# A fused graph and feed-forward kernel on one core: one-hots split over two engines, dead tiles dropped, loads and gathers started early

## The chip, the cores and the metric

The kernel runs on 1 core of one Trainium2 chip. The metric is the device time in microseconds (us) of one execution, from which the profile's span (first to last instruction) differs by the little that lies around it. Engines are named as in the profile: PE is TensorE, DVE VectorE, ACT ScalarE, POOL GpSimd, SP SyncE, which here only issues DMAs. ScalarE's and VectorE's instructions run in order on each engine, and the engines meet at semaphores and at a barrier between stages.

## The reference, cut to what matters

625 nodes with 768 features, 10000 edges sorted by destination, 34 relations. Four residual layers follow each other, each on a layer norm of the running `x`:

```python
x = x + gat_layer(elu(gat_layer(layernorm(x), heads=8)), heads=1)      # attention over all edges of a node
x = x + moe_ffn_0(layernorm(x))                                        # 8 experts, top 2
agg  = segment_sum(x[src], edge_type * n + dst); cnt = segment_sum(ones, ...)
mean = agg / maximum(cnt, 1)
h1   = einsum('rni,rio->no', mean, W_rel) + x @ W_root + b_rgcn        # x: layernorm(x)
xw   = h1 @ W_gcn                                                      # graph convolution:
x = x + dinv * segment_sum((xw * dinv)[src], dst) + xw * dinv**2 + b_gcn
x = x + moe_ffn_1(layernorm(x))                                        # 8 experts, top 2
```

The arithmetic on the weights is float16 in two parts: each float32 operand is cut into a high part and the rest ("hi" and "lo"), and each product is three products.

## The kernel before, in words

The 625 rows stand as NT = 5 tiles of 125 partitions. The stages follow each other with a barrier between them (`end_phase` or a block's end). Their starts, in us of the span, stand in the table of the next section.

**Edge stage** (`edge_phase`). The edges stand as 125 partitions x 80 columns. For each of 80 columns DVE makes two one-hots of 625 (`oh_s` from the sources at L207, `oh_d` from the destinations at L208, both in `hots`), in rings of HOTS = 8 that PE frees (`hots_free`), and PE (L352, L355, in `column`) multiplies them into a 625x625 matrix of edge counts and a count for each node and relation. Between the one-hots DVE works out where each edge goes (L223 to L286): the place of each edge in tiles of 128 edges, sorted by relation, with a second edge of the same pair beside the first (`ranks_ready` at L286). POOL then scatters one record for each edge column to DRAM (`scatter_records`, L392): TABLED_FIRST = 54 of the 80 in this stage, the others in the next. When PE's products are done, DVE stores counts (L291 to L294), makes the tables that steer the relation loop (L297 to L314: relation of each tile, whether a tile is the first of its relation, number of live turns), then masks (L318) and degrees (L319).

**Attention** (`gat_project`, `gat_attend`, twice). In the first projection SP loads the scattered records back when all 80 are written (L646), PE transposes them before its output tile 3 (`between`, L402), and DVE makes index columns from them (`slot_columns`). POOL gathers inverse counts beside all of the attention stages.

**The helper `Transposed`** is used in five places: for each row tile DVE normalises it (L517; for the norm it first takes `bn_stats` of all ten half tiles, L497), ACT writes the high part (L534), DVE the low part (L520), PE transposes both (L547), and ACT and DVE copy the result (L488, L486), in turns.

**Relation block** (`project_block` "q1", `relation_phase`, `gcn_phase`). q1 computes x @ W_root + bias; SP meanwhile stores the normalised rows to DRAM (`xn_dram`, L1845) and clears the accumulators. The relation loop then runs over tiles of up to 128 edges, in turns of UN = 4 tiles of which `live_turns` skips those that are dead as a whole. For each tile POOL gathers the rows of the edges' sources (L1559, L1561; AHEAD = 4 tiles ahead), PE sums rows of a tile that share a place (`mean`, L1700) and multiplies with the relation's weights (L599), ACT scales the result by the inverse count (L1628), POOL scatter-adds it to DRAM (L1579). A relation's weights (2304 KB) come through `wstage`, of two slots, and are cut into a ring by ACT (L1599) and DVE (L1640) at the first tile of the relation before. SP first waits for the first four gathers (L1537), then loads relation 1 (L1538). Relation 0 is loaded and cut already in q1 (`beside`). At the end SP loads both accumulators back (`load_sums`, 20 DMAs, L1867) before the stage may end. In `gcn_phase` DVE adds the halves (L510), PE multiplies with W_gcn and with the count matrix, and beside that the first weights of the last layer are merged in six chunks (`MergedFirst`: load, POOL L1463, DVE L1468 and L1470, ACT L1479, DVE L1474, which lets SP load the chunk after the next).

**Feed-forward layers** (`ffn_phase`, 0 and 1): router, gates, then up and down products.

## Time and profile before

| | |
|---|---|
| median of 3 runs | 1664.31 us (1662.63 to 1666.99) |
| the profiled execution | 1662.9 us, its span 1660.7 us |
| busy share of the span | PE 80%, PE weight loads 59%, DVE 56%, POOL 38%, ACT 32% |
| mean granted TensorE clock | 0.866 |

| stage | starts at, us |
|---|---|
| edge | 0 |
| first projection | 190.4 |
| rest of the attention | 254.2 |
| feed-forward 0 | 538.1 |
| q1 (root projection) | 729.6 |
| relation loop | 787.6 |
| graph convolution | 1356.8 |
| feed-forward 1 | 1452.8 |

How to read it: the busy shares are means over stages with different limits. In a timeline of an engine each row is one or more instructions, and the time in brackets behind it is the idle time before it and what ended that. An instruction's duration overlaps the next one's start on DVE and ACT by about 0.1 us, so a step is taken from start to start.

### The profile page before, as it was taken

The page shows a single profiled execution, that of the slowest core. Times are in us where ns is not written, and L with a number is a line of the kernel's source. Part 1 is how long each engine was busy: PE and PEld are TensorE (multiplying, and loading weights), DVE is VectorE, ACT ScalarE, POOL GpSimd, SP SyncE. Part 2 cuts the span into 40 slices and gives each one's busy share as a digit, 9 for nine tenths or more (in the row PEclk, how much of TensorE's full clock was granted, in tenths as well). Part 3 has the DMA queues.
Part 4 walks back from the last instruction along what each step waited for, and adds up shares of the span by engine and source line. Part 5 has one row for each costly group of instructions (what it writes and reads, how often), then busy time and mean ns, then how long its engine had stood idle before and what let it go on. Part 6 is the DMA issues. An engine that isn't in the chain of part 4 may idle for free. (4 is left out here: it accounts for less than half of the span.)

```text
span 1660.7 us, 30695 instructions
## 1 busy us (share of the span) xinstructions
PE 1335.1 (80%) x9640; PEld 982.2 (59%) x9641; DVE 935.8 (56%) x1711; ACT 535.8 (32%) x800; POOL 631.6 (38%) x751
## 2 busy tenths in 40 slices
PE   8699385792738489968599999999999938748988
PEld 6477365792634456856366666666666627435666
DVE  8953768685543644034266666566665536666810
ACT  0000320682320433013255554555555423122300
POOL 0077445776665000010355555555555522210000
PEclk9899685696769589988799999999999978958989
DMA  1000200000200421042699998899999865342301
GB/s 56 1 1 2 78 7 10 1 0 1 76 10 1 115 76 38 1 155 82 244 276 292 272 287 250 259 288 276 283 281 289 231 149 171 114 119 88 140 16 31
DMA packets 104209, 210.45 MB, mean 127 GB/s; under 512 B 23571, under 2 KB 48624, under 8 KB 104029
## 3 DMA queue, kind: packets, MB, share of 16 engines
q1 hardware_dynamic: 75484, 145.72, 25.5%
q0 software_dynamic: 28672, 64.04, 16.9%
q8 instruction: 32, 0.52, 0.1%
q14 instruction: 21, 0.16, 0.0%
HBM read 196.71 MB, written 37.22 MB: 141 GB/s over the span
## 5 line engine op out<-in xcount | busy, mean ns | idle before, releaser
L599 PE MATMUL r_pO<-ring,r_rowsT 128*128 x2592 | 433.1, 326 | 0.0
L599 PEld LDWEIGHTS r_pO<-ring,r_rowsT 128*128 128x128 f16 x2592 | 250.7, 98 | 158.4 <-issue 0.2
L1640 DVE SCALAR_TENSOR_TENSOR ring<-q_wstage,ring 128x768 f16<-128x768 f32 x198 | 175.2, 954 | 66.1 <-ACT ring L1599 61.9
L1579 POOL DMA_INDIRECT acc_dram<-r_msg,r_scol x72 | 133.0, 1847 | 167.0 <-PE r_pT L1700 98.0
L1599 ACT ACTIVATE ring<-q_wstage 128x768 f16<-128x768 f32 x198 | 148.8, 829 | 39.8 <-issue 25.0
L442 POOL DMA_INDIRECT inv_col<-qinv_dram,pair_col x112 | 120.0, 1072 | 79.3 <-POOL pair_col L455 74.4
L392 POOL DMA_INDIRECT slot_dram<-table_record,table_rowi x80 | 101.4, 1268 | 107.8 <-issue 107.2
L355 PE MATMUL acc<-oh_d,oh_s 125*125 125x512 f16 (+1 forms) x800 | 140.8, 316 | 0.0
L1628 ACT ACTIVATE r_msg<-r_pO,slot_inv 128x768 f32<-128x768 f32 x72 | 64.6, 897 | 191.6 <-PE r_pO L599 170.3
L1700 PE MATMUL r_pT<-r_S,q_parts 128*128 128x128 f16 x876 | 104.2, 222 | 24.2 <-DVE r_S L1657 12.6
L1647 DVE TENSOR_TENSOR r_rowsT<-r_pT,r_rowsT 128x512 f16<-128x512 f32 x73 | 50.2, 688 | 123.8 <-ACT r_rowsT L1608 111.7
L352 PE MATMUL acc<-R,oh_d 125*125 (+1 forms) x400 | 91.5, 229 | 18.8 <-DVE oh_d L208 18.8
L1700 PE MATMUL r_pT<-r_S,q_rows_b 128*128 128x128 f16 x876 | 104.3, 222 | 0.0
L887 PE MATMUL a_ps<-ident,cur 125*128 125x125 f32 x324 | 63.7, 371 | 49.0 <-ACT cur L861 23.5
L1559 POOL DMA_INDIRECT q_parts<-xn_dram,r_gcol x76 | 76.3, 1004 | 60.0 <-POOL r_gcol L1556 56.2
L1700 PEld LDWEIGHTS r_pT<-r_S,q_parts 128*128 128x128 f16 x876 | 70.8, 99 | 35.9 <-issue 27.9
L887 PEld LDWEIGHTS a_ps<-ident,cur 125*128 125x128 f32 x324 | 59.8, 286 | 52.8 <-ACT cur L861 23.2
L352 PEld LDWEIGHTS acc<-R,oh_d 125*125 125x125 f16 x400 | 56.3, 141 | 55.0 <-issue 19.3
L1561 POOL DMA_INDIRECT q_rows_b<-xn_dram,r_gcol x76 | 77.7, 1022 | 23.7 <-issue 23.1
L355 PEld LDWEIGHTS acc<-oh_d,oh_s 125*125 125x125 f16 x800 | 82.1, 144 | 0.0
L1329 DVE SCALAR_TENSOR_TENSOR x<-f_mps,x 125x384 f32<-125x384 f32 x20 | 10.2, 553 | 127.3 <-PE f_mps L599 127.3
L1556 POOL COPY r_gcol<-slot_idx 128x2 int32 (+1 forms) x76 | 58.0, 764 | 53.7 <-POOLq L1382 52.9
(359 smaller groups left out, 2421.0 us busy)
## 6 DMA issues: line engine op xcount, KB each, us to landing
q_wstage<-in_L_gnn_W_rel_dram SPq DMA_DIRECT2D x33, 2304.0 KB
f_stage<-in_L_ffn_w_dram SPq DMA_DIRECT2D x12, 768.0 KB, 5.1
stage<-in_L_gnn_W_dram SPq DMA_DIRECT2D x6, 768.0 KB
q_wstage<-in_L_ffn_w_fast_dram SPq DMA_DIRECT2D x6, 768.0 KB
q_wstage<-in_L_ffn_w_slow_dram SPq DMA_DIRECT2D x6, 768.0 KB
q_wstage<-in_L_ffn_h_fast_dram SPq DMA_DIRECT2D x6, 768.0 KB
f_stage<-in_L_ffn_w_fast_dram SPq DMA_DIRECT2D x6, 768.0 KB, 4.7
f_stage<-in_L_ffn_w_slow_dram SPq DMA_DIRECT2D x6, 768.0 KB, 6.2
```

Source lines behind the costliest of these rows:

```text
L352: eng.matmul(acc[0:P, 6, at:at + REL], oh_d[:, u, tile], onehot, start=False, stop=False, **kw)
L355: last = eng.matmul(a, oh_s[:, u, tile], oh_d[:, u, cols], start=False, stop=False, **kw)
L392: eng.indirect_dma_start(out=K.slot_dram, out_offset=bass.IndirectOffsetOnAxis(ap=K.table["rowi"][:, j:j + 1], axis=0), in_=K.table["recor ...
L442: eng.indirect_dma_start(out=got[:, u:u + 1], out_offset=None, in_=K.qinv_dram, in_offset=bass.IndirectOffsetOnAxis(ap=pair[:, u:u + 1], a ...
L599: ins = eng.matmul(out, x, w[:, h * n:(h + 1) * n], start=first and x is xh and w is wh, stop=last and x is xl, **kw)
L887: ins = eng.matmul(flat(bank)[:, lo:hi], bc(col[:, i:i + 1], [P, 128]), K.ident[0:P, off:off + hi - lo], start=True, stop=True)
L1559: eng.indirect_dma_start(out=rows[0][:, b, :], out_offset=None, in_=K.xn_dram, in_offset=bass.IndirectOffsetOnAxis(ap=gcol[:, b, 0:1], axi ...
L1561: eng.indirect_dma_start(out=rows[1][:, b, :], out_offset=None, in_=K.xn_dram, in_offset=bass.IndirectOffsetOnAxis(ap=gcol[:, b, 1:2], axi ...
L1579: eng.indirect_dma_start(out=K.acc_dram[u % 2], out_offset=bass.IndirectOffsetOnAxis(ap=scol[:, u:u + 1], axis=0), in_=msg[:, u, :], in_of ...
L1599: eng.activation(wring[:, slot, 0, k, :], wstage[:, slot, k, :], ACT.Copy, scale=W_SCALE).then_inc(s["w_hi"], 1)
L1640: ins_ = eng.scalar_tensor_tensor(wring[:, slot, 1, k, :], wstage[:, slot, k, :], W_SCALE, wring[:, slot, 0, k, :], ALU.mult, ALU.subtract)
L1700: last = eng.matmul(pT[b % 2][:, k // 4, (k % 4) * 128:(k % 4 + 1) * 128], rows[side][:, b, a * C + k * 128:a * C + (k + 1) * 128], S[:, b ...
```

## The change

Eight edits. (1) In the edge stage ACT makes `oh_d`, by a Square of (column number - destination) and a Relu of (1 - that), through a ring `apart` of four; DVE makes `oh_s` alone. The one-hots are spread differently between DVE's other steps, and the steering tables are made between one-hots, before the products end; degrees are reduced tile by tile; TABLED_FIRST is 46. (2) The live turns are two tiles and not four. (3) The statistics of the norm are taken by `measure` where rows of x are made (end of attention, of feed-forward 0 and of the graph convolution). (4) `Transposed` normalises tile i + 1 before it waits for tile i's high part. (5) Relation 1's and 2's weights are loaded, and the first four gathers made, in q1, where before they were made in the relation loop's stage. (6) `load_sums` loads tiles 0 and 1 in the relation stage and 2 to 4 in the next. (7) In the graph convolution the cuts of W_gcn stand between those of the rows on ACT and behind them on DVE. (8) The bias add of that stage goes from DVE to POOL.

```diff
-TABLED_FIRST = 54
+TABLED_FIRST = 46
@@ edge_phase, vector: hots
-                        eng.tensor_scalar(oh_s[:, u, :], iota_n[:, :], srcf[:, j:j + 1], None, ALU.is_equal)
-                        eng.tensor_scalar(oh_d[:, u, :], iota_n[:, :], dstf[:, j:j + 1], None, ALU.is_equal).then_inc(s["hots_ready"], 1)
+                        eng.tensor_scalar(oh_s[:, u, :], iota_n[:, :], srcf[:, j:j + 1], None, ALU.is_equal).then_inc(s["hots_s_ready"], 1)
...
-                hots(PREFIX_AT + 8, EJ)
+                hots(46, 52)
+
+                tg = c3[:, :].rearrange("p (t g) -> p t g", g=REL)
...
+                hots(60, EJ)
@@ edge_phase, scalar
+                def difference(j):
+                    eng.activation(apart[:, j % 4, :], iota_n[:, :], ACT.Square, bias=minus_dst[:, j:j + 1]).then_inc(s["apart_ready"], 1)
+
+                def hot(j):
+
+                    eng.wait_ge(s["hots_free"], j + 1)
+                    eng.wait_ge(s["apart_ready"], j + 1)
+                    eng.activation(oh_d[:, j % HOTS, :], apart[:, j % 4, :], ACT.Relu, scale=-1.0, bias=ones[0:EP, 0:1]).then_inc(s["hots_d_ready"], 1)
...
+                difference(0)
+                for j in range(1, EJ):
+                    difference(j)
+                    hot(j - 1)
@@ new
+def measure(K, eng, i):
+
+    for h in range(2):
+        last = eng.bn_stats(K.stats[:, i, h, :], K.x[:, i, h * HC:(h + 1) * HC])
+    return last
@@ Transposed.vector
+        prepare = add_halves if self.halves else normalise if self.norm else None
+        if prepare:
+            prepare(0)
         for i in range(NT):
-            if self.halves and i + 1 < NT:
-                add_halves(i + 1)
...
+            if prepare and i + 1 < NT:
+                prepare(i + 1)
             eng.wait_ge(s["hi_ready"], i + 1)
@@ relation_phase: live_turns, sync
-            turns = eng.value_load(K.live_row[0:1, TURNS:TURNS + 1], min_val=1, max_val=TURNS)
+            pairs = live_pairs(eng)
             with eng.Fori(1, TURNS) as i:
-                with eng.If(turns > i):
-                    for u in range(UN):
-                        step(i * UN + u, u, False)
+                for half in range(2):
+                    with eng.If(pairs > i * 2 + half):
+                        for u in (half * 2, half * 2 + 1):
+                            step(i * UN + u, u, False)
...
-            for b in range(AHEAD):
-                eng.wait_ge(gathered[b], 32)
-            load_w(eng, 1, 1)
-            with eng.Fori(1, REL // 2) as i:
+            eng.wait_ge(s["w_lo"], 2)
+            relation.load_w(eng, 3, 1)
+            with eng.Fori(2, REL // 2) as i:
...
-            load_sums(eng)
+            load_sums(eng, 0, 2)
@@ gcn_phase
+            load_sums(eng, 2, NT)
             eng.dma_start(bias[:, :], K.ins["L1_gnn_b_gcn"].partition_broadcast(P)).then_inc(s["bias_loaded"], 16)
...
-            merged.gpsimd(eng, 0, MERGE_CHUNKS)
+            merged.gpsimd(eng, 0, 2)
+            eng.wait_ge(s["bias_loaded"], 16)
+            eng.tensor_tensor(K.x[:, :, :], K.x[:, :, :], bc(bias[:, :].unsqueeze(1), [P, NT, C]), ALU.add).then_inc(s["bias_added"], 1)
+            merged.gpsimd(eng, 2, MERGE_CHUNKS)
...
-            W.scalar(eng)
-            T.scalar(eng)
+            T.scalar(eng, lambda i: W.scalar(eng, i, i + 1))
+            W.scalar(eng, NT)
@@ rgcn_phase: q1's sync and gpsimd
+            w_root.ready(eng, KC - 1)
+            relation.load_w(eng, 1, 1)
+            w_first.ready(eng, KC - 1)
+            relation.load_w(eng, 2, 0)
...
+            eng.wait_ge(s["dumped"], 48)
+            eng.wait_ge(s["extra"], 32)
+            T.wait_done(eng)
+            for b in range(AHEAD):
+                relation.gather(eng, b, b)
```

## Rows read from the trace of the kernel before

**Rows 1.** Relation loop: length, PE, PEld, DVE, ACT, POOL, PEclk, DMA, GB/s.
```profile
787.60:1356.80 569.20, 528.54 (x4418) 357.87 (x4418) 323.83 (x714) 273.65 (x416) 304.86 (x300) 0.97 0.90 265
```

**Rows 2.** Timeline of DVE, edge stage: start, duration, instruction, idle before.
```profile
84.72 0.24 DVE L286 TENSOR_TENSOR table_rowi<-place,beside 125x80 int32<-125x80 f32 x1
...
90.94 0.39 DVE L207 TENSOR_SCALAR oh_s<-iota_n,srcf 125x625 f16<-125x625 f16 x1 [0.70 <-PE acc L355]
...
154.91 0.38 DVE L207 TENSOR_SCALAR oh_s<-iota_n,srcf 125x625 f16<-125x625 f16 x1 [1.01 <-PE acc L355]
```

**Rows 3.** Timeline of PE, edge stage: a first product and the closing zeros.
```profile
9.36 0.76 PE L355 MATMUL acc<-oh_d,oh_s 125*125 125x512 f16 x2
...
168.19 1.68 PE L340 MATMUL acc<-zero 125*125 125x512 f16 x7
```

**Rows 4.** Timeline of ACT, attention: steps of 625, a table load.
```profile
300.67 1.28 ACT L847 ACT_TABLE_LOAD   x1
...
303.91 0.80 ACT L841 ACTIVATE t<-spread,al_s 125x625 f32<-125x625 f32 x1
304.62 0.71 ACT L847 ACTIVATE ex<-arg 125x625 f32<-125x625 f32 x1
```

**Rows 5.** Timeline of DVE (first three) and ACT (last), after the products.
```profile
171.59 4.06 DVE L297 TENSOR_TENSOR c<-iota_t,tin 128x3808 f32<-128x3808 f32 x1
...
183.30 2.58 DVE L318 TENSOR_SCALAR graph<-CT 125x625 bf16<-125x625 f32 x5
...
190.41 4.70 DVE L497 BATCH_NORM_STATS2 stats<-x 125x6 f32<-125x384 f32 x10 [1.09 <-PEq L90]
...
180.67 0.68 ACT L331 COPY CT<-acc 125x625 f32<-125x625 f32 x1 [1.00 <-PE acc L385]
```

**Rows 6.** Timeline of POOL: records scattered, the first, 54th, 55th and 80th.
```profile
85.98 4.61 POOL L392 DMA_INDIRECT slot_dram<-table_record,table_rowi  x1 [81.33 <-issue]
...
171.00 1.19 POOL L392 DMA_INDIRECT slot_dram<-table_record,table_rowi  x1 [0.31 <-issue]
...
191.27 1.19 POOL L392 DMA_INDIRECT slot_dram<-table_record,table_rowi  x1 [0.64 <-POOL h L653]
...
231.16 1.19 POOL L392 DMA_INDIRECT slot_dram<-table_record,table_rowi  x1 [0.30 <-issue]
```

**Rows 7.** Timeline of PE, first projection: transposes of the loaded tables.
```profile
236.36 0.74 PE L402 MATMUL g_ps<-ident,table_tables 112*128 112x112 f32 x4 [1.82 <-DMA table_tables<-slot_dram]
```

**Rows 8.** Timeline of ACT, feed-forward 0: the last copy of its row transposes.
```profile
559.01 1.48 ACT L488 COPY f_xT<-f_ps 128x750 f16<-128x750 f16 x2 [2.53 <-PE f_ps L547]
```

**Rows 9.** Timeline of DVE in q1, of POOL (fourth gather) in the loop.
```profile
768.48 1.83 DVE L1856 TENSOR_TENSOR q_h<-q_h,q_bias 125x768 f32<-125x768 f32 x2 [5.22 <-DMA xn_dram<-q_parts]
...
799.83 1.01 POOL L1561 DMA_INDIRECT q_rows_b<-xn_dram,r_gcol  x1 [0.30 <-issue]
```

**Rows 10.** Timeline of PE, relation loop: first row, third and last tile.
```profile
798.79 0.37 PE L1700 MATMUL r_pT<-r_S,q_parts 128*128 128x128 f16 x2 [10.90 <-DMA q_rows_b<-xn_dram,r_gcol]
...
829.58 6.16 PE L599 MATMUL r_pO<-ring,r_rowsT 128*128 x36
...
1334.48 6.01 PE L599 MATMUL r_pO<-ring,r_rowsT 128*128 x36
```

**Rows 11.** Timeline of SP's queue: the loads of the sums, first and last.
```profile
1347.95 0.83 SPq L1867 DMA_DIRECT2D q_h<-acc_dram  x2
...
1355.50 0.79 SPq L1867 DMA_DIRECT2D q_xn<-acc_dram  x2
```

**Rows 12.** Timeline of DVE and of POOL, graph convolution.
```profile
1378.34 4.15 DVE L1787 TENSOR_TENSOR x<-x,q_bias 125x3840 f32<-125x3840 f32 x1
...
1388.81 3.55 DVE L1474 SCALAR_TENSOR_TENSOR ring<-q_wstage,ring 128x1536 f16<-128x1536 f32 x1 [2.74 <-ACT ring L1479]
...
1387.99 2.75 POOL L1463 TENSOR_TENSOR q_wstage<-q_wstage,gate 128x1536 f32<-128x1536 f32 x1 [28.35 <-DMA q_wstage<-in_L_ffn_h_fast_dram]
```

**Rows 13.** Timeline of DVE, feed-forward 1: a wait for a load.
```profile
1483.72 0.55 DVE L1126 TENSOR_SCALAR f_b2p<-f_early 8x768 f16<-8x768 f32 x1 [7.92 <-DMA f_emb<-in_L_ffn_router_emb_dram]
```

209 lines of the change are left out of this document (119 added, 90 removed).

## The prediction, made before the changed kernel ran

> **What bounds the kernel now.** I read the windows by stage first, then each engine's timeline around the edits. In the edge stage one column of PE's products takes (154.91 - 90.94) / 38 = 1.683 us, and DVE waits for PE there [rows 2]; 80 columns are 134.6 us, yet the products end at 169.87 [rows 3], because earlier in the stage DVE's ranking steps starve PE. Behind them the stage lasts until 190.4, on DVE [rows 5]. In the first projection PE waits for tables that POOL's scatter delivers [rows 6, 7]. The relation loop is PE's, busy 528.5 of 569.2 us [rows 1], with 10.9 us lost at its start and more before its third tile [rows 10]. The stages around it are chains of small steps in which no engine is full: there each step on the chain costs its whole length.
>
> **Edge stage.** After the change PE is fed by DVE's one instruction and ACT's two a column. ACT's nearest rows of 625 elements start 0.71 us apart where the bias is a column [rows 4]; two are 1.42 us, below PE's 1.683, so PE sets the pace. The ring of 8 holds 13.5 us of PE's work, more than any of DVE's steps between two groups of one-hots. From the first product at 9.36, the products' end is 9.2 + 134.6 + 2.4 + 0.5 + 1.7 = 148.4: 2.4 for PE's half pace in the first 5 us (0.76 us a pair [rows 3]), 0.5 for the prefix products, 1.7 for the zeros. That is 21.5 us earlier. The table step from 171.59 to 183.30 [rows 5] moves between one-hots, where DVE has idle time. The masks then wait for the last count transpose, 181.35 - 169.87 = 11.5 us after the products [rows 5]; masks and degrees are 190.41 - 1.09 - 183.30 = 6.0 us for five tiles, so 1.2 follow the last. The next stage starts at 148.4 + 11.5 + 1.2 + 1.1 = 162.2, not 190.4: **-28.2**.
>
> **What POOL makes of that.** 80 records take (171.00 - 85.98) / 53 = 1.60 us each [rows 6]. ranks_ready at 84.96 [rows 2] comes at about 80: DVE saves 32 oh_d ahead of it and makes 14 oh_s more, and now sometimes waits for PE's ring (bounds 79 and 85). 46 records end at 81 + 46 x 1.6 = 155, hidden under 162.2 by 7 us; if that cover were gone, each us would count. In the projection 34 records and not 26 remain. The tables' transposes came 236.36 - 190.4 = 46.0 after the stage's start, 5.2 after the 80th record [rows 6, 7]; now 0.9 + 33 x 1.6 + 5.2 = 58.9: **+12.9**. PE's wait there grows from 1.8 to about 15 to 18 us, and after such a gap it starts at half pace: between 0 and the 2.4 above, I take 1.8. So 28.2 - 14.7 = **-13.5** for both stages: the edge stage's gain is given back in half, because POOL's chain of records only moves by its earlier start and by the shorter hole between its 54th and 55th (171.00 to 191.27).
>
> **Statistics and order of normalising.** The ten bn_stats are 4.70 us at the head of three stages [rows 5]. Moved, each tile's 0.94 lies under PE's products, except the last: +1.1 with its wait, three times. Feed-forward 0: the chain of transposes ended 559.01 + 1.48 - 538.1 = 22.4 us after the start [rows 8]. Without the statistics what is late next is ACT's table load of 1.28 [rows 4] (0.4 of it shows) and, before PE's first transposes, POOL's selection mask (it eats 1.3); the new order, in which the tile after is normalised while ACT writes this one's high part, gives 1.3 back. So 4.7 - 0.4 - 1.3 + 1.3: **-4.3** (bounds -3 and -6), +1.1 at the end of the attention. q1: 4.7 - 0.4 + 1.3, no mask: **-5.6** (bounds -4 and -6.5), +1.1 at feed-forward 0's end. Feed-forward 1: **0**, since DVE waits until 1483.72, 31 us into the stage, for a load that SP's queue delivers no sooner [rows 13].
>
> **q1 takes four gathers and two loads.** The rows' store lands at 768.5 [rows 9], some 5 us earlier once shifted; the four gathers take 800.84 - 787.6 = 13.2 us [rows 9] and end at 777 to 782, where q1 now ends at 782. Two loads of 2304 KB on SP's queue stand behind that store, not before it. Nothing shows: 0, bounds 0 and +5.
>
> **Relation loop.** The third tile's products began 829.58 - 787.6 = 42.0 us after the stage's start [rows 10], behind the gathers (10.9), the load of relation 1 that waited for them, and its cuts. With both there, the first products begin 5 us in (select, sums, cuts of the rows) and the third's two tiles on, at 19.6: **-22.4** (bounds -15 and -24). A tile is (1334.48 - 829.58) / 69 = 7.3 us [rows 10], tile 71 being the last. Counting the inputs as the kernel does gives 32 relations of two tiles and two of three: 70 live, so 35 pairs: **-14.6**. The second branch per turn lies under 36 queued products: 0. At the end 20 loads are issued in 8.3 us [rows 11]; eight take 3.3: **-5.0**.
>
> **Graph convolution.** DVE's first cuts of W_gcn go behind the rows, so PE's products start 4 us earlier (12 issues of loads now in front may take 1 back). What ends the stage is the chain of merged chunks: it loses the 4.15 us bias add [rows 12] and gains three statistics, 2.8, but starts 2.5 earlier, as W_gcn is cut earlier: **-3** (bounds -6 and +4). On POOL the add has 3840 columns, by the row of 1536 in 2.75 us [rows 12] 6.9 us. A row speaks against it: DVE's cut at 1388.81 takes 3.55 us and ends 1.6 us after POOL's multiply does [rows 12], so DVE stood still for POOL. The Trainium skill ("SBUF — State Buffer", section "Who interferes with whom") says that a DVE instruction with two SBUF inputs and a GpSimd one that reads SBUF exclude each other for the whole instruction; the trace agrees. One cut then waits up to 5 us, and the load it releases is needed only after PE's first products with the counts, so I count 0 for it.
>
> **Sum.** -28.2 + 14.7 + 1.1 - 4.3 + 1.1 - 5.6 - 22.4 - 14.6 - 5.0 - 3.0 = -66.2. Span 1660.7 - 66.2 = 1594.5; the profiled execution lay 2.2 above its span, and the median of the runs 1.4 above that: 1598, rounded down to 1597.
>
> **Rivals.** (A) Start of the relation loop: gathers, weight loads and the store of h1, which POOL's first scatter waits for, fall together; q1 ends 5 late and a third of the 22.4 is lost: 1597 + 5 + 7 = 1609. For it: the DMA share is 0.90 in the loop [rows 1]. Against: the window of q1 has queues free after the store. (B) ACT becomes the bound of the products: from a pair of 1.683 on. At 2.0 it is 80 x 0.32 = 25, in part under POOL: 1617. Against: [rows 4]. (C) POOL's bias add lies on the merge chain: +7 in place of -3: 1607. (D) Slower: Square and Relu do not share an activation table, and each column reloads twice: 2 x 1.28 + 1.42 = 3.98 us [rows 4], 80 x 2.3 = +184: 1781. It decides above 1.683 + 66 / 80 = 2.5 us a column, so one reload (2.70) is enough, 1678. No row shows a Square; for sharing speaks that Identity and Exp alternate after one load [rows 4]. The Trainium skill ("ScalarE: Activation LUTs", section "Table sets: the hidden batching unit") counts cheap functions such as relu in every set and doesn't name square there. (E) The pairs do nothing, as 71 or 72 tiles live: 1611.
>
> **Chances.** Forecast, 1589 to 1605: 0.62. Below 1589 (all upper bounds at once): 0.09. A 0.12, C 0.08, B 0.05, D 0.03, E 0.01. The range 1586 to 1614 leaves out D, most of B and the edge below. A measurement can tell 0.3% (5 us): faster 0.96, same 0.01, slower 0.03.
>
> **What would show it.** Right: products ending near 148 with PE's columns at 1.68 us, ACT's pairs at 1.4 and no table load between; the first projection starting at 162 and PE waiting 15 to 18 us for the tables; 70 scatters; the third tile's products 20 us into the relation loop; feed-forward 1 of unchanged length. Wrong: PE waiting for oh_d, DVE still for POOL in the graph convolution while a load is due, gathers landing after the loop's start.

## The result and the profile after

The changed kernel takes 1622.44 us (median of 4 runs, 1620.95 to 1628.56) beside 1665.65 us for the kernel before on the same chip: a ratio of 0.9748 with a 95% interval of 0.9717 to 0.9780. The profiled execution took 1621.38 us, its span is 1619.6 us, 41.1 less than before, where 66.2 were forecast. The time lies outside the range of 1586 to 1614.

The head of the page after, and the window of the relation loop (columns as in [rows 1]):

```profile
span 1619.6 us, 30896 instructions
PE 1317.4 (81%) x9518; PEld 968.5 (60%) x9519; DVE 919.3 (57%) x1626; ACT 649.5 (40%) x954; POOL 633.4 (39%) x744
771.98:1308.27 536.29, 513.72 (x4296) 347.50 (x4296) 319.50 (x700) 270.75 (x410) 290.11 (x280) 0.98 0.90 264
```

The same engines are as busy as before; ACT has gained 8 points of share from its one-hots. By stage (lengths in us; the last column is the best kernel of the experiments below, on another chip, in the longest of its six executions):

| stage | before | forecast change | after | change | combined kernel |
|---|---|---|---|---|---|
| edge | 190.4 | -28.2 | 160.7 | -29.7 | 162.8 |
| first projection | 63.9 | +14.7 | 78.6 | +14.7 | 66.2 |
| rest of the attention | 283.9 | +1.1 | 284.9 | +1.0 | 286.5 |
| feed-forward 0 | 191.5 | -3.2 | 190.0 | -1.5 | 190.0 |
| q1 | 58.0 | -5.6 | 57.8 | -0.2 | 54.7 |
| relation loop | 569.2 | -42.0 | 536.3 | -32.9 | 529.3 |
| graph convolution | 96.0 | -3.0 | 101.8 | +5.9 | 94.2 |
| feed-forward 1 | 207.9 | 0 | 209.5 | +1.6 | 212.0 |
| span | 1660.7 | -66.2 | 1619.6 | -41.1 | 1595.7 |

So the stages up to feed-forward 0 came out nearly as forecast, and four places behind them did not: the root projection, the start and the end of the relation loop, and the graph convolution. The lines follow, each answering to rows of before.

**Edge stage and first projection** (against [rows 3], [rows 4], [rows 6], [rows 7]). Timelines of PE, ACT (six rows), POOL and again PE:

```profile
144.22 1.68 PE L369 MATMUL acc<-zero 125*125 125x512 f16 x7
...
5.27 1.28 ACT L338 ACT_TABLE_LOAD   x1 [5.11 <-DVE minus_dst L219]
...
22.13 0.80 ACT L344 ACTIVATE oh_d<-apart,ones 125x625 f16<-125x625 bf16 x1
...
23.54 0.80 ACT L344 ACTIVATE oh_d<-apart,ones 125x625 f16<-125x625 bf16 x1
...
61.93 0.82 ACT L344 ACTIVATE oh_d<-apart,ones 125x625 f16<-125x625 bf16 x1
62.65 0.81 ACT L338 ACTIVATE apart<-iota_n,minus_dst 125x625 bf16<-125x625 f16 x1
63.62 0.82 ACT L344 ACTIVATE oh_d<-apart,ones 125x625 f16<-125x625 bf16 x1 [0.16 <-PE acc L385]
...
214.15 1.19 POOL L422 DMA_INDIRECT slot_dram<-table_record,table_rowi  x1 [0.30 <-issue]
...
219.47 1.02 PE L432 MATMUL g_ps<-ident,table_tables 112*128 112x112 f32 x4 [15.13 <-DMA table_tables<-slot_dram]
```

The products end at 145.9 and not at 169.9; there is one table load and none between Square and Relu. Early in the stage, while the ring of one-hots has free places, ACT takes 1.41 us from one Relu to the next (22.13 to 23.54); once the ring is full it takes 1.69 (61.93 to 63.62) and waits for PE in each. So PE sets the pace, with a margin of some 0.27 us, as worked out. The 80th record starts 53.5 us after the projection's start, and PE waits 15.13 us for the tables.

**Root projection** (against [rows 5]). Timelines of POOL and DVE at its head, two rows of after and three of before:

```profile
714.15 5.22 POOL L1912 MEMSET q_rows_b<- 128x6144 f16 x1 [185.17 <-POOLq L90]
...
714.89 4.50 DVE L539 TENSOR_SCALAR q_sd<-q_mv 125x5 f32<-125x5 f32 x1
```

```profile
729.62 5.22 POOL L1850 MEMSET q_rows_b<- 128x6144 f16 x1 [186.84 <-POOLq L90]
...
729.66 4.70 DVE L497 BATCH_NORM_STATS2 q_stats<-x 125x6 f32<-125x384 f32 x10 [0.99 <-PEq L90]
...
734.98 0.17 DVE L502 TENSOR_SCALAR q_sd<-q_mv 125x5 f32<-125x5 f32 x1
```

A DVE step on five columns takes 4.50 us and ends as POOL's memset does. Before, the ten bn_stats lay over that memset, in the same 4.70 us that they take without one, and the step on five columns came behind both, in 0.17 us. The bn_stats were taken away, and what they had covered is on the path.

**Start of the relation loop** (against [rows 10]). Timelines of PE, POOL and DVE from the fourth tile on:

```profile
800.00 6.01 PE L639 MATMUL r_pO<-ring,r_rowsT 128*128 x36
809.58 0.27 PE L1754 MATMUL r_pT<-r_S,q_parts 128*128 128x128 f16 x2 [3.58 <-DVE r_S L1711]
...
811.20 7.46 PE L639 MATMUL r_pO<-ring,r_rowsT 128*128 x36
...
791.58 1.64 POOL L1634 DMA_INDIRECT acc_dram<-r_msg,r_scol  x1 [12.47 <-DMA acc_dram<-q_h]
...
801.21 0.22 DVE L1721 SCALAR_TENSOR_TENSOR r_scol<-r_dup,row_move,row_base 128x1 int32<-128x1 f32 x1 [5.32 <-DMA acc_dram<-r_msg,r_scol]
802.65 5.34 DVE L1694 SCALAR_TENSOR_TENSOR ring<-q_wstage,ring 128x768 f16<-128x768 f32 x6 [1.23 <-issue]
```

The third tile's products begin 20.8 us into the stage (forecast 19.6). Then one step of PE is 11.20 us and the next 8.69, for 7.25: 5.4 us too much. Read backwards: PE waits for DVE's selection, which stands behind the cut of relation 2 at 802.65, which stands behind a column that waits for the landing of the first scatter, which waited 12.47 us for the store of h1.

**End of the loop** (against [rows 10], [rows 11]). Timelines of PE, POOL, SP's queue and DVE:

```profile
1284.44 6.01 PE L639 MATMUL r_pO<-ring,r_rowsT 128*128 x36
...
1292.35 1.62 POOL L1634 DMA_INDIRECT acc_dram<-r_msg,r_scol  x1 [2.29 <-ACT r_msg L1682]
...
1300.32 0.79 SPq L1934 DMA_DIRECT2D q_xn<-acc_dram  x2
...
1308.27 0.17 DVE L1837 TENSOR_SCALAR q_dinv<-deg 125x5 f32<-125x5 f32 x1 [20.25 <-PEq L1564]
```

SP has issued its eight loads by 1301.1, but the next stage starts at 1308.2. From the start of the last tile's product it is 23.8 us, where it was 22.3 with 20 loads: 12 loads fewer gained nothing.

**Graph convolution** (against [rows 12]). Timelines of POOL, DVE and PE:

```profile
1343.39 8.30 POOL L1814 TENSOR_TENSOR x<-x,q_bias 125x3840 f32<-125x3840 f32 x1
...
1343.53 9.78 DVE L1515 TENSOR_TENSOR q_wstage<-q_wstage 128x1536 f32<-128x1536 f32 x1 [2.71 <-POOL q_wstage L1508]
...
1355.81 7.74 PE L639 MATMUL n_ps<-q_gcn_parts,q_parts 128*125 128x384 f16 x36 [4.32 <-ACT q_xn L1829]
...
1394.63 8.28 PE L1870 MATMUL n_ps<-q_xn,graph 125*125 125x384 f32 x20 [3.08 <-DVE x L1852]
```

DVE's add, 1.76 us elsewhere, takes 9.78 us: it stands still for POOL's 8.30, and PE waits behind it. PE waits once more, 3.08 us, before its last tile, whose 20 products then take 8.28 us at a granted clock of 0.81; before they took 6.71 at 1.00, behind a wait of 0.25.

**Feed-forward 1** (against [rows 13]) still waits for the same load, now 11.84 us long:

```profile
1441.75 0.55 DVE L1168 TENSOR_SCALAR f_b2p<-f_early 8x768 f16<-8x768 f32 x1 [11.84 <-DMA f_emb<-in_L_ffn_router_emb_dram]
```

### The profile page after: what moved, and what is told of

Read it like the earlier page. It is cut to its first block and busy times, and to the rows that moved or that the text cites. A ratio compares the mean times of both kernels' runs of the same rounds, so it can differ in the third digit from the quotient of the medians.

```text
span 1619.6 us, 30896 instructions
## 1 busy us (share of the span) xinstructions
PE 1317.4 (81%) x9518; PEld 968.5 (60%) x9519; DVE 919.3 (57%) x1626; ACT 649.5 (40%) x954; POOL 633.4 (39%) x744
## 5 line engine op out<-in xcount | busy, mean ns | idle before, releaser
L639 PE MATMUL r_pO<-ring,r_rowsT 128*128 x2520 | 422.4, 327 | 0.0
L639 PEld LDWEIGHTS r_pO<-ring,r_rowsT 128*128 128x128 f16 x2520 | 244.2, 98 | 154.9 <-issue 1.5
L1634 POOL DMA_INDIRECT acc_dram<-r_msg,r_scol x70 | 131.0, 1871 | 152.5 <-PE r_pT L1754 101.8
L472 POOL DMA_INDIRECT inv_col<-qinv_dram,pair_col x112 | 120.1, 1073 | 79.2 <-POOL pair_col L485 73.6
L385 PE MATMUL acc<-oh_d,oh_s 125*125 125x512 f16 (+1 forms) x800 | 134.9, 308 | 0.0
L1754 PE MATMUL r_pT<-r_S,q_parts 128*128 128x128 f16 x852 | 100.4, 221 | 4.5 <-DVE r_S L1711 4.4
L927 PE MATMUL a_ps<-ident,cur 125*128 125x125 f32 x324 | 60.5, 358 | 50.9 <-ACT cur L901 24.2
L1754 PE MATMUL r_pT<-r_S,q_rows_b 128*128 128x128 f16 x852 | 100.5, 221 | 0.0
L1550 POOL DMA_INDIRECT q_parts<-xn_dram,q_gcol x74 | 74.4, 1005 | 57.2 <-POOL q_gcol L1546 55.5
L1552 POOL DMA_INDIRECT q_rows_b<-xn_dram,q_gcol x74 | 75.9, 1026 | 22.6 <-issue 22.6
L1912 POOL MEMSET q_rows_b<- 128x6144 f16 x1 | 5.2, 5217 | 185.2 <-POOLq L90 185.2
```

The source lines that it names most:

```text
L385: last = eng.matmul(a, oh_s[:, u, tile], oh_d[:, u, cols], start=False, stop=False, **kw)
L472: eng.indirect_dma_start(out=got[:, u:u + 1], out_offset=None, in_=K.qinv_dram, in_offset=bass.IndirectOffsetOnAxis(ap=pair[:, u:u + 1], a ...
L639: ins = eng.matmul(out, x, w[:, h * n:(h + 1) * n], start=first and x is xh and w is wh, stop=last and x is xl, **kw)
L927: ins = eng.matmul(flat(bank)[:, lo:hi], bc(col[:, i:i + 1], [P, 128]), K.ident[0:P, off:off + hi - lo], start=True, stop=True)
L1550: eng.indirect_dma_start(out=self.rows[0][:, b, :], out_offset=None, in_=self.K.xn_dram, in_offset=bass.IndirectOffsetOnAxis(ap=self.gcol[ ...
L1552: eng.indirect_dma_start(out=self.rows[1][:, b, :], out_offset=None, in_=self.K.xn_dram, in_offset=bass.IndirectOffsetOnAxis(ap=self.gcol[ ...
```

## The experiments

They ran on four chips, numbered 1, 4, 5 and 12 here; on which one the two kernels above ran is not known. The kernel before ran beside them each time, with medians of 1666.3 to 1676.9 us. The two kernels also went to chip 4, unaltered.

**The two kernels on chip 4.**

> The changed kernel unaltered, beside the kernel before, on the chip of these runs. Theory (this chip differs from the first in places that both kernels have): the edge stage's products end some 15 us later than 145.9, single tiles of the relation loop take 8.1 to 8.4 us for 7.25, the ratio is 0.98 and not 0.9748; the steps at the start of the relation loop (11.2 and 8.7 us), DVE's 4.50 us at the head of the root projection, the 23.8 us from the last tile's product to the graph convolution and its length of 102 us are the same as on the first chip. Rival (the experiments' own edits made the edge stage and the loop slower): 160.7 and 7.25 us again, 1622 us.

> The kernel before, unaltered, one look. If this chip is slower for PE while POOL scatters records, its edge stage is longer too, by less than the changed kernel's 15 us, as PE has 21 us of products less on its path there; the relation loop is 569 us or, where tiles take over 8 us, up to 585.

Measured: 1647.96 us (1629.67 to 1652.47) for the changed kernel, ratio 0.984 (0.977 to 0.991); the kernel before, profiled, has an edge stage of 204.0 us, 13.7 more than above, a loop of 570.1 and a graph convolution of 99.0, 3.0 more than above. The changed kernel's profiled execution is the shortest of its four and has 163.5, 79.8, 286.1, 189.7, 57.7, 537.8, 103.2 and 210.0 us for its eight stages; its products end at 149.3, 3.4 us later than above and not 15. The steps named above are the same or close: 12.0 and 8.2 us at the loop's start, 4.49 us at q1's head, 23.8 us at the loop's end.

Two things come and go in the profiled executions, and neither is in the result above. The first is the edge stage: 174 to 179 us in all eight kernels on chip 1 and in two more on chip 4, but 159 to 164 in the unaltered one there and in the four on chips 5 and 12. The kernel before has it too. The second is a stretch in the relation loop, from about the 41st tile to the 64th, in which every other step of PE is 8.0 to 8.4 us for 7.25, some 11 us in all. Seven experiments have it: tables behind the fifth tile, h1 tile by tile, both of the graph convolution, the constants, the first combined kernel and the last one. Four others on chip 1, the two unaltered kernels on chip 4 and the three kernels on chip 5 don't have it. In it ACT's copy of the next tile starts late; timelines of ACT, in the run with h1 stored tile by tile and in the one with the zeros in the edge stage:

```profile
1130.63 0.58 ACT L1661 CAST r_rowsT<-r_pT 128x512 f16<-128x512 f32 x1 [3.19 <-DMA stage<-in_L_gnn_W_dram]
```

```profile
1122.40 0.58 ACT L1666 CAST r_rowsT<-r_pT 128x512 f16<-128x512 f32 x1 [0.28 <-PE r_pT L1759]
```

The cause of either was not found, and no kernel was profiled twice, so that they may go with the execution or with the program. For the whole times it means this: apart from the combined kernels and the turns of four, eight of the nine altered kernels lie at ratios of 0.979 to 0.981, with intervals that overlap that of the unaltered 0.984, and only the one with the tables moved (0.970) is told apart. What follows is therefore read from single stages and steps, and by ratios only in the batch of the combined kernels on chip 5, where neither thing shows in a profile.

**Tables behind the fifth tile.** Does POOL's chain of records hold the first projection?

```diff
-            def between(i): if heads > 1 and i == 3: turn_tables(...)
-            project_tiles(eng, pO, B["xT"], W, between, ...)
+            project_tiles(eng, pO, B["xT"], W, lambda i: None, ...)
+            if heads > 1: turn_tables(...)
```

> The changed kernel with the transposes of the loaded tables behind the first projection's fifth output tile on PE (they stand before the fourth), and DVE's index columns behind its products of the fifth tile. Theory (15.1 us of PE's wait before the fourth tile are POOL's chain of records, which the earlier end of the edge stage didn't shorten, and two tiles of products can lie under it): the stage is 66 to 69 us and not 78.5, 10 to 12 us less, that is most of what the prediction booked as given back. Rival (DVE's index columns and products behind the tables set the end either way): less than 4 us are won.

Measured: the projection is 66.4 us, for 77.7 to 79.2 in the runs of that chip without the edit, and the ratio is 0.970 (0.965 to 0.974). PE's wait is down to 3.32 us in its timeline:

```profile
232.46 0.73 PE L432 MATMUL g_ps<-ident,table_tables 112*128 112x112 f32 x4 [3.32 <-DMA table_tables<-slot_dram]
```

The theory holds: some 12 us of the 14.7 that were booked as given back by POOL were a wait that two tiles of products can cover. The rest of the attention is 286.7 us in this run, for 284.6 to 285.2 in the same others, so that up to 2 us may come back behind it; the last combined kernel has the same edit and 285.1.

**q1: whose 4.50 us?** First the zeros of the gathered rows on DVE, in the hole before its first cut, with the clears of the accumulators (SP stores the same zeros to DRAM) behind the rows' store:

```diff
-            eng.memset(rows_b[:, :, :], 0.0).then_inc(s["zeroed"], 1)          # gpsimd
+            eng.memset(rows_b as 128x3072 float32, 0.0).then_inc(s["zeroed"], 1)   # vector, behind T.vector
```

> The changed kernel with the zeros of the gathered rows written by DVE (as 128x3072 float32, in the 2.86 us in which it waits for ACT's first cut of the weights) instead of by POOL at the head of the root projection; SP stores the rows before the zeros. Theory (POOL's memset of 5.22 us holds DVE's step of 125x5, 4.50 us for 0.17, and so eats the statistics that were moved away): that step is 0.17 us, PE's first transposes come 4.3 us earlier, and the stage is 53 to 55 us and not 57.8; if DVE's zeros take longer than the hole, up to 1.5 us of it is given back: 1618 to 1620 us. Rival (the step's 4.50 us are ACT's table load or a wait of DVE's own that the row hides): the step stays near 4.5 us and the time 1622 us.

Measured: q1 is 60.5 us, longer than the 57.7 of the unaltered kernel, and yet its head is as the theory has it. Timelines of DVE and POOL:

```profile
730.51 0.17 DVE L539 TENSOR_SCALAR q_sd<-q_mv 125x5 f32<-125x5 f32 x1
...
771.69 0.19 POOL L1547 COPY q_gcol<-slot_idx 128x2 int32<-128x2 int32 x1 [227.13 <-DMA acc_dram<-q_rows_b]
```

The step is 0.17 us, with ACT's table load still beside it. But the clears now came later, and the gathers, which wait for them, began 41.9 us into the stage and not 39.9. The edit had moved a DMA together with the instruction that releases it, the very thing to look out for. So the clears went to the edge stage, where the queue is empty:

```diff
+        (DVE's memset as above)
+                for flat in (acc_dram[0] rows N.., acc_dram[1]): 14 stores of empty[:, 0:384]   # edge stage, SP
-            three stores of the zeroed rows                                                     # q1, SP
```

> The changed kernel with the accumulators cleared in the edge stage, from a tile that is zero there anyway, and the zeros of the gathered rows written by DVE in the root projection while it waits for ACT's first cut. With the clears left in the root projection DVE's step of 125x5 fell from 4.50 to 0.17 us, but the clears moved behind the rows' store and held the gathers until 42 us into the stage, so that it was 60.5 us. Theory (head of the stage held by POOL's memset, end by PE's products): the stage is 53 to 54 us and not 57.8. The rows' store, beside less traffic, lands in under 22 us. Rival (the rows' store or the gathers behind it set the end once the head is short): 56 to 58 us.

Measured: q1 is 53.5 us, 4.2 less than unaltered. The theory holds.

**Start of the loop: h1 stored tile by tile.**

```diff
-            eng.dma_start(acc_dram[0][0:N], h1).then_inc(s["seeded"], 16)        # relation stage
+            for i in range(NT):                                                  # q1, SP
+                eng.wait_ge(s["rooted"], i + 1)
+                eng.dma_start(K.acc_dram[0][i * P:(i + 1) * P, :], h1[:, i, :]).then_inc(relation.s_seeded, 16)
```

> The changed kernel with h1 stored tile by tile while the root projection makes it (five stores of 375 KB, each behind its bias add) and not by one store of 1875 KB at the start of the relation stage, which landed 19.6 us after its issue. Theory (that store holds POOL's first scatter until 791.6, behind it the gathers and DVE's scatter column of the fifth tile at 801.2, and so DVE's cut of relation 2 and PE): the first scatter starts within 2 us of its message (786), PE's step of 11.2 us behind the fourth tile becomes 7.3, the next one of 8.7 too, and the loop is 5.4 us shorter: 1617 us. If the stores slow the gathers or the loads of relations 1 and 2 in the root projection, up to 2 us of it are lost there. Rival (the fifth tile is late because relation 3's load or cut is late whatever the scatters do): PE still waits 3 to 4 us before it, 1622 us.

Measured: PE's step behind the fourth tile is 7.77 us and the next 36 are within 0.4 of 7.25, and POOL's first scatter starts 14.1 us into the stage, straight behind its message, for 19.6. Timeline of POOL:

```profile
806.62 2.06 POOL L1634 DMA_INDIRECT acc_dram<-r_msg,r_scol  x1 [6.83 <-PE r_pT L1754]
```

4.9 of the 5.4 us are regained; q1 was 2.7 us longer in this run (60.4), where up to 2 were allowed for, so that 2.2 are left. The loop as a whole is 542.6 us, because the stretch of long steps lies in it. The store was the cause of the first long steps. Relation 3's load (the rival) was not.

**End of the loop.** Four kernels. Where nothing else is said, the times are from the start of the last tile's product to the next stage. The second pair's branch inside the first's:

```diff
-                for half in range(2):
-                    with eng.If(pairs > i * 2 + half): two steps
+                with eng.If(pairs > i * 2):
+                    two steps
+                    with eng.If(pairs > i * 2 + 1): two steps
```

> The changed kernel with one edit: in each turn of the relation loop the second pair's branch stands inside the first pair's, so that a turn with both pairs dead meets one branch and not two. 70 tiles live, so the last 10 of 28 turns are dead as a whole: 21 branches not taken become 11. Theory (the loop's end is set by the dead branches): PE's last product ends at 1290.45 and the next stage starts 17.75 us later though SP issued its last load of the sums at 1301.1; the branches take 17.75 / 21 = 0.85 us each. With 11 the engines are through 9 to 10 us after PE's last product, SP's loads come last again, and the stage of the graph convolution starts 6 to 7 us earlier: 1622 - 6.5 = 1615.5 us. Rival (the end waits for gathers of dead tiles to land, or for anything else that is not a branch): the gap of 7.1 us between SP's last issue and the next stage stays, 1622 us.

Measured: 21.8 us for 23.8. Ten branches not taken fewer are 2.0 us, 0.2 us each and not 0.85: the theory named a part and took it for the whole. Then no dead turn at all:

```diff
-            with eng.Fori(1, TURNS) as i: ...
+            turns(1, 18)
+            with eng.If(pairs > 36): turns(18, TURNS)
```

> The changed kernel with the relation loop's turns in two loops: turns 1 to 17, and behind one branch (more than 36 pairs live) turns 18 to 27, which are dead here. In the run with the second pair's branch inside the first's, ten branches fewer shortened the way from the last tile's product to the next stage from 23.8 to 21.8 us, 0.2 us each. Theory (a dead turn costs some 1.3 us for the loop's own step besides its branches, and that now sets the loop's end): without ten dead turns SP's loads of the sums come last, and the way from the last tile's product's start to the next stage is 17.2 us (the last load's issue ended 16.7 behind that start) and not 23.8: 6.6 us less. Rival (what is left is POOL's wait for the gathers of dead tiles or the barrier itself): 21 to 24 us as before.

Measured: 20.9 us for the 17.2 of the theory, so the ten dead turns with one branch each are only 0.9 more. The theory falls. POOL, SP's queue and DVE in its timelines:

```profile
1309.50 1.62 POOL L1638 DMA_INDIRECT acc_dram<-r_msg,r_scol  x1 [2.24 <-ACT r_msg L1686]
...
1317.78 0.79 SPq L1938 DMA_DIRECT2D q_xn<-acc_dram  x2
...
1322.51 0.17 DVE L1841 TENSOR_SCALAR q_dinv<-deg 125x5 f32<-125x5 f32 x1 [17.34 <-PEq L1564]
```

3.9 us lie between SP's last issue (1318.6) and the stage, 13.0 between POOL's last scatter and DVE's first instruction of the stage. Next, POOL's waits against registers, with their numbers for these edges in their place:

```diff
-                eng.wait_ge(scattered[a], pairs * 16)
+                eng.wait_ge(scattered[a], 35 * 16)
-                eng.wait_ge(gathered[u], times[u // 2] * 32)
+                eng.wait_ge(gathered[u], (19, 18)[u // 2] * 32)
```

> The changed kernel with the turns in two loops (no dead turn runs) and the numbers of these edges (35 pairs; 19 and 18 gathers of a buffer) written into the last waits of POOL and SP in place of registers loaded from memory. Without dead turns the next stage started 12.9 us after POOL's last scatter, 3.9 us after SP's last load; in the kernel before it was 14.4 us with SP's 20 loads over it, so that this path lay hidden. Theory (POOL's register loads and waits against registers make the path long): the next stage starts 9.5 to 10.5 us after the last scatter, right behind SP's loads, and is up to 3.4 us earlier. Rival (it is the landing of the scatter and gathers plus POOL's own end of a block): 12.9 us stay.

Measured: 12.6 us behind the last scatter for 13.0, where up to 3.4 less were expected; it is not the registers. Last, in the combined kernel (below), POOL leaves at once and SP does the waiting:

```diff
             load_sums(eng, 0, 2)
+            for u in range(AHEAD): eng.wait_ge(gathered[u], (19, 18)[u // 2] * 32)   # SP
-            six waits and a nop                                                       # gpsimd
```

> The combined kernel with the last waits of the relation stage on SP alone: POOL leaves the stage behind its last scatter and first multiply, and SP, which waits for the scatters anyway, waits for the last gathers too (their numbers, 19 and 18, written in). In the combined kernel the next stage starts 21.8 us after the last tile's product, 12.5 to 12.9 us after POOL's last scatter began, and some 4 us after SP's last load. Theory (POOL's own way out of a block, about 5 us behind its last work, stands behind the landing of the scatter, and the 20 loads of the kernel before lay over it): now it runs beside the landing, SP's loads come last, the next stage starts 9.5 to 10 us after the last scatter and is 3 us earlier; the ratio falls from 0.953 by 0.002. Rival (the barrier or SP's own end needs the 4 us): 12.5 to 12.9 us stay, 0.953.

Measured: 19.3 us from the last product to the next stage, where the combined kernel has 21.8; 11.4 us behind the last scatter for 13.9. POOL, SP's queue and DVE:

```profile
1281.74 1.62 POOL L1645 DMA_INDIRECT acc_dram<-r_msg,r_scol  x1 [2.27 <-ACT r_msg L1687]
...
1289.72 0.79 SPq L1932 DMA_DIRECT2D q_xn<-acc_dram  x2
...
1293.12 0.17 DVE L1839 TENSOR_SCALAR q_dinv<-deg 125x5 f32<-125x5 f32 x1 [2.94 <-PEq L1569]
```

The stage ends 2.5 us earlier, nearly as the theory has it (3). This run has the stretch of long steps (a loop of 538.5 us for 529.3), and its ratio (0.955, 0.952 to 0.958) can't be told from the combined kernel's. So POOL's way out of the stage was the last wait; what in it takes the time was not separated. Nor was what remains: the stage starts 2.6 us behind SP's last issue and 2.9 behind DVE's bias add, which the combined kernels have there.

**Graph convolution.** The bias add back on DVE:

```diff
-            merged.gpsimd(eng, 0, 2); POOL's bias add; merged.gpsimd(eng, 2, MERGE_CHUNKS)
+            merged.gpsimd(eng, 0, MERGE_CHUNKS)
+            link(eng.tensor_tensor(K.x, K.x, bias, ALU.add))          # vector, ahead of the first chunk
```

> The changed kernel with the bias add of the graph convolution back on DVE, where it stood before, ahead of the first merged chunk. Theory (POOL's add of 8.30 us locks DVE's add of two SBUF operands for its whole length: 9.78 us for 1.76, and POOL's multiply of chunk 2 starts behind it): the chain of chunks regains about 8 us and pays DVE's 4.15 us, so that the stage is 95 to 98 us and not 101.9: 1616 to 1619 us. Rival (the stage got longer by the three statistics in the chain and by loads of the sums that stand in front): those stay, the DVE add comes on top, and the stage is 102 to 106 us: 1622 to 1626 us.

Measured: the stage is 99.5 us. The six other runs of that chip that leave the stage alone have 102.6 to 106.3, three of them 103.2 or 103.3; in the result above it was 101.8. PE's wait of 4.32 us amid its products is gone, the one before its first product with the counts has grown from 1.14 to 3.24, and that of 3.08 us before its last tile stays: 2.3 to 3.7 us are won, a part of the 8.9 that the stage missed. Then the statistics too:

```diff
+        (as above)
-                measure(K, eng, i)                                                  # graph convolution
+        norm = {"measured": layer == 0, ...}                                        # feed-forward 1 takes them itself
```

> The changed kernel with the bias add of the graph convolution back on DVE and, too, the statistics of the last norm back at the head of feed-forward 1. With the bias add alone back the stage took 99.5 us, PE still waited 3.08 us for DVE before its last tile, and that tile's 20 products took 8.3 us for 6.7, the clock having fallen in the wait. Theory (the three statistics in the chain of merged chunks make that wait; at the head of feed-forward 1 they cost nothing, since DVE waits there for a load until 31 us): the graph convolution is 94 to 96 us, feed-forward 1 within 0.5 us of its length, together 6 to 8 us less than the changed kernel. Rival (the wait comes from the chunks' loads or from POOL's multiplies that block DVE): 98 to 100 us with the wait of 3 us still there, and feed-forward 1 pays up to 4.7.

Measured: 96.0 us, and feed-forward 1 is 209.4 us, with the ten bn_stats at its head and still 9.57 us of wait in front of the same step. Timeline of DVE:

```profile
1431.41 4.70 DVE L497 BATCH_NORM_STATS2 stats<-x 125x6 f32<-125x384 f32 x10 [1.27 <-PEq L90]
...
1462.65 0.55 DVE L1168 TENSOR_SCALAR f_b2p<-f_early 8x768 f16<-8x768 f32 x1 [9.57 <-DMA f_emb<-in_L_ffn_router_emb_dram]
```

The two edits together are worth 7.3 us against the unaltered 103.2 of this chip, number 4, where the kernel before has 99.0. PE's wait before its last tile is 1.77 us here, and the tile takes 6.7 us at a granted clock of 1.00, for 8.3 us at 0.81.

**All of it.** A first combined kernel, with the statistics of the first norm in the edge stage besides, and those of the last still in the graph convolution:

> The changed kernel with all of it: turns in two loops, h1 stored tile by tile, clears in the edge stage, tables transposed behind the fifth output tile, the statistics of the first norm in the edge stage while DVE waits for the products, and in the relation stage's last 15 us, in which DVE and POOL wait, the bias add (DVE) and POOL's first multiply of the merged weights. Theory by stages against the changed kernel: first projection -4.5 -11, root projection -4.3, start of the relation loop -5.4, its end -6 (DVE's add of 4.2 us lies before 1301), graph convolution -9 (no blocked adds): 40 us less than the changed kernel, 5.0% below the kernel before on a chip where that one is 2.5% below. Rivals: the adds and the multiply now block each other at the loop's end and give 3 to 5 us back; the chain of merged chunks keeps the graph convolution at 98 us or more.

Measured: 0.966 (0.961 to 0.971), 1617.5 us, where 0.950 was expected; its profile has both the long edge stage (178.7 us) and the stretch of long steps. By stages the gains of the single runs are there (67.0, 54.1 and 98.6 us for first projection, q1 and graph convolution), except that the statistics in the edge stage give nothing: the projection waits for the tables anyway. Without them, and with the last norm's statistics back at the head of feed-forward 1:

> The changed kernel with what the runs showed to gain: tables transposed behind the fifth output tile, clears in the edge stage and the gathered rows' zeros on DVE, h1 stored tile by tile, turns in two loops, the bias add on DVE at the end of the relation stage, POOL's first multiply there too, and the last norm's statistics at the head of feed-forward 1. Theory, by the single runs against the changed kernel: -12.1 -4.3 -5.4 -3 -7 = -32 us, a ratio near 0.96 where the changed kernel has 0.984 on this chip. Rival (the run with all edits but the last had 0.966; the statistics of the last norm are hidden beside the chain when the bias add is gone): 0.966 again.

Measured: 1589.76 us (1587.75 to 1597.75, 6 runs), ratio 0.953 (0.9517 to 0.9543), which beats both kernels, and 0.96 was expected. The head of its page:

```profile
span 1595.7 us, 30673 instructions
PE 1315.2 (82%) x9518; PEld 968.2 (61%) x9519; DVE 911.0 (57%) x1628; ACT 650.3 (41%) x954; POOL 614.2 (38%) x742
```

All 70 tiles of its loop stand 7.25 us apart within 0.4; no step is long.

**Are two dead tiles worth 14.6 us?** Turns of four again, in the changed and in the combined kernel:

```diff
+                (the number of live pairs rounded up to an even one)
-                for half in range(2): with eng.If(pairs > i * 2 + half): two steps
+                with eng.If(pairs > i * 2): four steps
```

> The changed kernel with turns of four tiles again and one branch for each, so that 72 tiles run for 70. Theory (two tiles are worth 14.6 us, and the second branch per turn costs nothing): the relation loop is 13 to 16 us longer than the changed kernel's, its ratio 0.993 where that one has 0.984. Rival (the branch per two tiles costs PE something in each turn, and most of all in the stretches of 8.1 to 8.4 us per other tile, where ACT starts each pair of tiles some 2 us late): less than 10 us are lost, down to nothing where such a stretch is long.

> The first kernel of this batch with turns of four tiles. Theory (pairs are worth two tiles): 14 us slower than it. Rival (stretches of slow pairs eat that): within 5 us of it.

Measured: 72 tiles run in both. The loop is 544.5 us for 529.3 in the combined kernel, whose whole time is 1606.18 us against 1589.76 in the same batch, 16.4 more, ratio 0.9636 (0.9623 to 0.9649). In the changed kernel it is 549.5 us, for 536.3 on the first chip and 537.8 on chip 4; its ratio is 0.981 (0.980 to 0.983), beside 0.975 on the first chip and not the 0.993 that was expected beside chip 4's 0.984. None of these loops has the stretch of long steps. So the pairs bring what two tiles cost. The second branch per turn costs nothing that shows in a live turn; in the dead ones it is the 2.0 us of the loop's end, which turns of four are spared (21.9 for 23.8). The rival falls.

## Why the prediction was wrong, step by step

**Right.** The edge stage (-28.2 forecast, -29.7 measured): the products end 2.5 us sooner than worked out, and what follows them takes 1.0 more. The first projection: +14.7 and +14.7, PE's wait 15.13 us within "15 to 18". The end of the attention: +1.1 and +1.0. The pairs: 70 scatters, 13 to 16 us by the undoing runs for 14.6. The third tile 20.8 us into the loop for 19.6. Rivals A (as far as it says that gathers or loads collide), B, D and E did not come: ACT's Square and Relu run behind one table load, 1.41 us a pair where nothing holds them, for the 1.42 that was worked out.

**q1: -5.6 forecast, -0.2 measured.** The step that failed is "q1: 4.7 - 0.4 + 1.3, no mask". There was no mask, but POOL's memset of 5.22 us stands at the same place, and the ten bn_stats had lain over it. The prediction asked what was late next behind the statistics and looked only at ACT and at the mask. The runs put it at 4.2 of the 5.4 us that are missing; the other 1.2 stay open. The Trainium skill ("SBUF — State Buffer", section "Who interferes with whom") lists tensor_scalar among the DVE steps that can want the port pair shared with GpSimd, and says that whichever of the two issues first has the pair for its whole instruction while the other is blocked. The 4.50 us beside a memset agree, and so do DVE's 3.15 us for 1.27 at the head of feed-forward 0:

```profile
525.78 1.46 POOL L1145 TENSOR_SCALAR_AFFINE_SELECT f_sel<-f_sel 8x1536 f16<-8x1536 f16 x1
...
526.24 3.15 DVE L549 TENSOR_SCALAR f_wparts<-x,f_mv,f_sd 125x768 f32<-125x768 f32 x2
```

There the mask had been allowed for: PE's first product of the router comes 3.75 us earlier, for 4.3. Of the 1.7 us by which that stage missed, 0.6 is this. Another 1.0 is PE's first group of products behind the gates: 8.52 us at a granted clock of 0.64, where before it took 7.55 at 0.72.

**The loop's start: 5.4 us.** The -22.4 for the third tile's products "at 19.6" is right to 1.2 us, but the path was followed on PE's side alone, and only as far as that tile. The store of h1 was named in rival A as what POOL's first scatter waits for, and given no price of its own. It lands 19.7 us after its issue. Before, the loop's late start covered it: the first scatter began at 825.3, 37.3 us after the store's issue, behind its message; once the start came 21 us earlier, that cover was gone. SP's queue and POOL before, and SP's queue after:

```profile
787.98 0.28 SPq L1535 DMA_DIRECT2D acc_dram<-q_h  x1
...
825.27 1.64 POOL L1579 DMA_INDIRECT acc_dram<-r_msg,r_scol  x1 [20.39 <-ACT r_msg L1628]
```

```profile
771.92 0.30 SPq L1602 DMA_DIRECT2D acc_dram<-q_h  x1
```

The run with five stores gives 4.9 us of it back. Against the table's -32.9 for -42.0 the loop's misses are 1.2 and 5.4 us here and 6.5 at its end; 4.0 come the other way. From the third tile to the last the mean step is 7.34 us over 67 steps; without the 5.4 us it is 7.26, where [rows 10] gave 7.32, since that mean had three long steps in it (8.57, 8.25 and 8.12 us).

**The loop's end: -5.0 forecast, +1.5 measured.** The step that failed is to count the loads taken away as a gain: that 20 loads are issued in 8.3 us and "eight take 3.3" is right, and SP was through 0.5 us before the stage's end in the kernel before. What was not asked is what stood under the 20 loads. Two things: dead turns and their branches (2.9 us by two runs), and POOL's way from its last scatter to the end of the stage, 12.6 to 13.0 us without dead turns; if it was as long before, it was over some 1 us before SP's last issue ended, 13.9 us behind that scatter (POOL before, beside [rows 11]), and so lay hidden:

```profile
1342.39 1.63 POOL L1579 DMA_INDIRECT acc_dram<-r_msg,r_scol  x1 [2.28 <-ACT r_msg L1628]
```

The run that takes POOL's waits away gains 2.5. Together 5.4 of the 6.5 us.

**Graph convolution: -3 forecast, +5.9 measured.** PE's products do start 2.85 us earlier (18.0 us into the stage for 20.9), as worked out. Behind that start 4.4 us more go by until the first product with the counts, 3.6 more until the last tile, and 1.6 more in that tile. Rival C, a bias add on POOL that lies on the merge chain, was near this case; it had a chance of 0.08 and a price of 10 us against the forecast, and the stage missed by 8.9. POOL's add itself took 8.30 us for the 6.9 worked out. The step that failed is "one cut then waits up to 5 us, and the load it releases is needed only after PE's first products with the counts, so I count 0 for it": the instruction that waited was not a cut but the add behind it, it waited 8.0 us, and what stood behind it was ACT's next cut and, behind that on ACT, the copy of z for which PE waits. The cost of a blocked instruction was looked for in what it releases, and not in what stands in line behind it. The row that spoke against the edit ([rows 12], 3.55 us) was read, and its weight was put aside. Besides, the statistics were 2.8 us on the same chain and were moved there from feed-forward 1, where DVE "waits until 1483.72" and so nothing could be gained for them: the prediction had both facts, in two places. Taking both edits back gives 7.3 us.

**Left open.** Feed-forward 1's 1.6 us (its load lands 31.6 us into the stage for 30.9, which is 0.7 of it), 1.2 us of q1, what POOL does at the end of a stage, and the cause of the long edge stage and of the stretch of long steps.

## What to carry to other kernels

When a step on the path is taken away or moved, list everything that ran beside it on the other engines, with its end time: the gain ends at the first of these ends, and three of the four misses here were such a cover (a memset under statistics, a store under a late start, an engine's way out of a stage under 20 loads). A large wait that an edit leaves in place (15 us for a table) is worth a look at what could run in it, which gave more here than any of the four misses. Moving an elementwise step to an idle POOL is not free while DVE works on SBUF operands: here an add of 8.30 us on POOL stopped DVE's add for 8.0, and what stood in DVE's queue with it. And before two runs are compared by their whole times, compare the stages that the edit doesn't touch: here they moved by more than the edits did.

## What the runs showed of the hardware

- POOL held DVE to the end of its instruction in tensor_scalar, even of five columns (4.50 us for 0.17 beside a memset of 5.22), and in an add of two SBUF operands (9.78 for 1.76 beside an add of 8.30). It didn't hold bn_stats: ten take 4.70 us beside that memset and without it.
- From the start of POOL's last scatter to the next stage it is 12.6 to 13.9 us when POOL waits for its landing (15.9 where ten dead turns with 21 branches follow); with SP doing the waiting 11.4.
- A branch not taken costs some 0.2 us (2.0 us for ten), where the loop is over for every engine.
- One store of 1875 KB from 125 partitions lands 19.7 us after its issue, some 97 GB/s, with the DMA engines 0.25 to 0.47 busy meanwhile; in five pieces, issued as they are ready, it is off the loop's path and costs the stage before 2.7 us.
- 80 Squares and 80 Relus alternate on ACT behind one table load, 0.80 us each for 625 columns and 1.41 us from pair to pair.
- The edge stage of the changed code was 159 to 164 us in some profiled executions and 174 to 179 in others, on chip 4 both; the kernel before had 190.4 and 204.0.
- The same 20 products took 6.71 us at a granted clock of 1.00, behind waits of 0.25 and 1.77 us, and 8.28 us at 0.81 behind a wait of 3.08.
